# Softmax layers of a graph network: dense products from two float32r parts, four dense regions, and the border between gathered and dense nodes at 2750 in place of 3250

## What is computed

```python
msg = jax.nn.relu(x[src]) + EPS_MSG
m = jax.ops.segment_max(msg, dst, num_segments=n)
ex = jnp.exp(msg - m[dst])
alpha = ex / segment_sum(ex, dst, n)[dst]
out = segment_sum(msg * alpha, dst, n) + x
h = batch_norm(out @ W1 + b1);  x = relu(relu(h) @ W2 + b2)
```

## Time and profile before

| | |
|---|---|
| median of 3 runs | 4451.83 us (4436.73 to 4454.9) |
| the profiled execution | 4460.21 us, span 4458.4 us |
| TensorE, its weight loads | 3626.2 us (81%), 2451.3 us (55%) |
| GpSimd | 2568.9 us (58%) |
| VectorE, ScalarE | 1998.9 us (45%), 1185.7 us (27%) |
| DMA | 744.31 MB, 167 GB/s |
| setup, until the first gather | 749 us |
| softmax layers 1, 2, 3 with their nodes stages | 749 to 1478, 2230, 3006 us, about |
| edge layers | 3006 to 4425 us, about |

### The profile page before, as it was taken

The page is one execution under the profiler, slowest core; times in us unless marked ns, Lnnn a source line. Parts: engine busy times, 40 slices in busy tenths (PEclk is TensorE's granted clock), DMA queues, the critical chain, the costliest instruction groups (busy, mean ns, idle before and its releaser), DMA issues. The chain is left out here.

```text
span 4458.4 us, 73923 instructions
## 1 busy us (share of the span) xinstructions
PE 3626.2 (81%) x22631; PEld 2451.3 (55%) x22631; DVE 1998.9 (45%) x5297; ACT 1185.7 (27%) x2569; POOL 2568.9 (58%) x2700
## 2 busy tenths in 40 slices
PE   2588887889897888999687989876788788878887
PEld 0355554545555544555554555575666666666665
DVE  6354433122223712131641222374566666666666
ACT  1232111000001500000420000173444444444444
POOL 4566554556664665666475666536556565555552
PEclk6798988999998989999898999897898989899888
DMA  6365445666664766666376666464444444444442
GB/s 244 119 203 166 135 137 171 199 192 210 206 216 126 242 196 192 215 208 203 123 252 191 203 206 215 152 189 132 115 126 126 123 129 123 125 125 126 123 128 66
DMA packets 347311, 744.31 MB, mean 167 GB/s; under 512 B 73666, under 2 KB 177276, under 8 KB 346339
## 3 DMA queue, kind: packets, MB, share of 16 engines
q0 software_dynamic: 134912, 331.04, 25.7%
q1 hardware_dynamic: 204295, 358.83, 25.1%
q10 hardware_dynamic: 7899, 51.90, 3.0%
HBM read 608.06 MB, written 133.44 MB: 166 GB/s over the span
## 5 line engine op out<-in xcount | busy, mean ns | idle before, releaser
L603 POOL DMA_INDIRECT ring<-split_table,src_idx x1240 | 1179.4, 951 | 735.0 <-issue 334.9
L1488 PE MATMUL ps<-spare,acc 128*128 128x500 fp8e4 x5292 | 1229.3, 385 | 201.1 <-issue 97.9
L2117 POOL DMA_INDIRECT ring<-h_table,idx_ring x832 | 822.3, 988 | 581.2 <-issue 276.1
L1488 PEld LDWEIGHTS ps<-spare,acc 128*128 128x128 bf16 x5292 | 521.0, 100 | 850.0 <-issue 280.2
L1589 DVE TENSOR_TENSOR onehot<-onehot,ps 128x168 f32<-128x168 f32 x165 | 54.3, 329 | 1268.9 <-PE ps L1499 775.0
L616 POOL DMA_INDIRECT adjacency<-acc x408 | 403.0, 988 | 308.3 <-issue 112.8
L1433 ACT ACTIVATE work<-ps 84x256 f32<-84x256 f32 x155 | 58.9, 380 | 1744.1 <-remote 1305.2
L1520 PE MATMUL ps<-ring,onehot 128*84 128x256 bf16 x3720 | 469.1, 281 | 47.1 <-issue 46.3
L1520 PEld LDWEIGHTS ps<-ring,onehot 128*84 128x84 bf16 x3720 | 416.0, 122 | 73.5 <-issue 69.5
L2127 PE MATMUL ps<-ident,ring 128*128 128x128 f32 x1664 | 296.7, 302 | 99.0 <-issue 74.1
L2166 PEld LDWEIGHTS ps<-mats,work 128*128 128x128 f32 x1664 | 244.8, 208 | 167.7 <-issue 166.1
(11 more groups left out here) (328 smaller groups left out, 4920.3 us busy)
## 6 DMA issues: line engine op xcount, KB each, us to landing
acc<-split_table SPq DMA_DIRECT2D x104, 768.0 KB
spare<-adjacency SPq DMA_DIRECT2D x108, 512.0 KB
e_few<-spare SPq DMA_DIRECT2D x104, 512.0 KB
acc<-e_few SPq DMA_DIRECT2D x208, 256.0 KB
work<-in_edge_attr SPq DMA_DIRECT2D x104, 256.0 KB
split_table<-acc ACTq DMA_DIRECT2D x32, 768.0 KB
ring<-split_table,src_idx POOLq DMA_INDIRECT x1240
adjacency<-Z ACTq DMA_DIRECT2D x6, 3136.0 KB
```

The costliest lines, as they stand in the source:

```text
L603: e.indirect_dma_start(out=to, out_offset=None, in_=table, in_offset=bass.IndirectOffsetOnAxis(ap=src_idx[:, 2 * i + h, j:j + 1], axis=0)) ...
L1488: ins = e.matmul(ps[2 + 2 * c + kind][:, 0:width], split[j % 2][:, k, q, kind * D:(kind + 1) * D], moving, start=(b == q == 0), stop=(b == ...
L2117: e.indirect_dma_start(out=rows[:, s, j, :], out_offset=None, in_=h_table, in_offset=bass.IndirectOffsetOnAxis(ap=idx_ring[:, s, j:j + 1], ...
```

## The change

- The border goes to 2750: 46 pairs in place of 55, 250 nodes at a time as before; the dense part has 3500 nodes in four regions, of 1000, 1000, 1000 and 500. Setup scatters 476 columns in place of 408 and zeroes half a region more.
- The dense products no longer use the split table. ScalarE casts a block's counts from fp8 to float32r (`cast_block`, five buffers) and makes exp(x - c) of two blocks at a time (`dense_exp`), VectorE multiplies (`dense_times`), ScalarE rounds to a float32r high part (`dense_high`), VectorE subtracts to get the low part. TensorE multiplies 2 kinds x 2 parts per chunk: 8 matmuls for a block of 1000 columns, 4116 in the kernel.
- ScalarE and VectorE do this at the end of each step for the blocks of the next one. TensorE's blocks start at step 4 and fill 4130 columns a step.
- SyncE loads plain rows (256 KB a unit) in place of the split rows (768 KB), behind `d_mul`, and counts behind `cast`. In layers 2 and 3 the first dense work waits for the whole split table and its stores (`space_made`), since it takes over their memory.
- The gathered pairs keep the split table and their three bf16 parts.

```diff
-CUT = 3250
-PAIRS = 55
+CUT = 2750
+PAIRS = 46
 WHOLE = 5
 SLOTS3 = 3
-GROUP0 = 106
+GROUP0 = 89
 COLS = (NG - GROUP0) * J
...
-REGIONS = [(0, [500, 500]), (1000, [500, 500]), (2000, [500, 500])]
-STEP_BLOCKS = 2.75
+REGIONS = [(0, [500, 500]), (1000, [500, 500]), (2000, [500, 500]), (3000, [500])]
+CHUNKS = sum(len(widths) for _, widths in REGIONS)
+DUOS = -(-BLOCKS // 2)
+CASTS = 5
+FIRST_STEP = 4
+STEP_COLUMNS = 4130
...
 
-    return max(0, int((n - 3) / STEP_BLOCKS))
+    r, b = divmod(n, BLOCKS)
+    before = sum(BLOCKS * sum(widths) for _, widths in REGIONS[0:r]) + b * sum(REGIONS[r][1])
+    return FIRST_STEP + before // STEP_COLUMNS
...
+                            whole_rows = sum(REGIONS[r][1]) > PITCH // 2
+                            if whole_rows:
+                                e.dma_start(adjacency[at:at + half, :].rearrange("(p x) o -> p (x o)", p=P),
+                                            Z0[:, 0:half // P // 4].bitcast(U8)).then_inc(S("zero_fill"), 16)
+                            else:
+                                half_rows = adjacency[r * SPAN * PITCH:r * SPAN * PITCH + NR * PITCH, :].rearrange("(p b d) o -> p b (d o)", b=BLOCKS, d=PITCH)
+                                at = slice(h * BLOCKS // 2, (h + 1) * BLOCKS // 2)
+                                zeros = Z0[:, 0:(at.stop - at.start) * PITCH // 8].bitcast(U8).rearrange("p (b d) -> p b d", d=PITCH // 2)
+                                e.dma_start(half_rows[:, at, 0:PITCH // 2], zeros).then_inc(S("zero_fill"), 16)
...
+            def space_made(e, S):
+                if not ready:
+                    e.wait_ge(S("v_low"), UNITS)
+                    for b in range(5):
+                        e.wait_ge(S(f"split_out{b}"), stored_units(max(u for u in range(UNITS) if made_in(u) == b)))
...
+                    width = sum(REGIONS[r][1])
+                    if j >= 2:
+                        e.wait_ge(S("cast"), last_block(j - 2))
...
+                def load_dense_rows(j):
+                    u = j % UNITS
                     n = blocks_of(u)
-                    reached(e, S("dense"), j - 1)
-                    if not ready and j < 4:
-                        e.wait_ge(S(f"split_out{j - 2}"), 16)
-                    if not ready and r == 0:
-                        e.wait_ge(S(f"split_out{made_in(u)}"), stored_units(u))
-                    e.dma_start(split[j % 2][:, 0:n, :, :].rearrange("p n q x -> p n (q x)"), split_by_block[:, u * UNIT:u * UNIT + n, :]
-                                ).then_inc(S(f"split_in{j % 2}"), 16)
-
+                    if j >= 2:
+                        e.wait_ge(S("d_mul"), duos_through(j - 2))
+                    e.dma_start(dense_rows[j % 2][:, 0:n, :], by_block[:, u * UNIT:u * UNIT + n, :]).then_inc(S(f"dense_rows_in{j % 2}"), 16)
...
+                def dense_exp(d):
+                    n = first_block(d)
+                    j, k = unit_of(n), n % BLOCKS % UNIT
+                    m = end_block(d) - n
+                    if d == 0:
+                        space_made(e, S)
+                    if k == 0:
+                        e.wait_ge(S(f"dense_rows_in{j % 2}"), 16 * (j // 2 + 1))
+                    reached(e, S("d_low"), d - 1)
+                    e.activation(dense_values[d % 2][:, 0:m, 0:D], dense_rows[j % 2][:, k:k + m, :], ACT.Exp, bias=negc[:, :]
+                                 ).then_inc(S("d_exp"), 1)
+
+                def dense_high(d):
+                    m = end_block(d) - first_block(d)
+                    e.wait_ge(S("d_mul"), d + 1)
+                    if d >= 2:
+                        e.wait_ge(S("dense"), end_block(d - 2))
+                    e.activation(two_parts[:, d % 2, 0:m, 0, :], dense_values[d % 2][:, 0:m, :], ACT.Copy).then_inc(S("d_high"), 1)
+
+                def cast_block(n):
+                    r = n // BLOCKS
+                    j, k = unit_of(n), n % BLOCKS % UNIT
+                    width = sum(REGIONS[r][1])
+                    if k == 0:
+                        e.wait_ge(S(f"counts_in{j % 2}"), 16 * (j // 2 + 1))
+                    reached(e, S("dense"), n - CASTS + 1)
+                    e.activation(cast_counts[n % CASTS][:, 0:width], counts[j % 2][:, k, 0:width].bitcast(F8), ACT.Copy).then_inc(S("cast"), 1)
+
+                def keep_products(r):
+                    for c, width in enumerate(REGIONS[r][1]):
+                        e.wait_ge(S("dense"), BLOCKS * (r + 1))
+                        reached(e, S("evacuated"), 2 * (r - 1) + c + 1)
+                        e.activation(products[c][:, 0:width], ps[3 + 2 * c][:, 0:width], ACT.Copy).then_inc(S("product_kept"), 1)
+
+                def dense_duo(d):
+                    if d == 0:
+                        dense_exp(0)
+                    if d + 1 < ALL_DUOS:
+                        dense_exp(d + 1)
+                    if d > DUOS and d % DUOS == 1:
+                        keep_products(d // DUOS - 1)
+                    cast_block(first_block(d))
+                    dense_high(d)
+                    for n in range(first_block(d) + 1, end_block(d)):
+                        cast_block(n)
+
                 if not ready:
                     exp_rows(0)
...
+                    d = r * DUOS + b // 2
+                    e.wait_ge(S("d_low"), d + 1)
...
+                            for q in range(2):
+                                ins = e.matmul(ps[2 + 2 * c + kind][:, 0:width], two_parts[:, d % 2, b % 2, q, kind * D:(kind + 1) * D],
+                                               cast_counts[n % CASTS][:, at:at + width], start=(b == q == 0), stop=(b == BLOCKS - 1 and q == 1))
                         at += width
-                    if k == blocks_of(u) - 1:
-                        ins.then_inc(S("dense"), 1)
+                    ins.then_inc(S("dense"), 1)
...
+                def dense_times(d):
+                    n = first_block(d)
+                    j, k = unit_of(n), n % BLOCKS % UNIT
+                    m = end_block(d) - n
+                    e.wait_ge(S("d_exp"), d + 1)
+                    e.scalar_tensor_tensor(out=dense_values[d % 2][:, 0:m, D:2 * D], in0=dense_rows[j % 2][:, k:k + m, :], scalar=EPS_MSG,
+                                           in1=dense_values[d % 2][:, 0:m, 0:D], op0=ALU.add, op1=ALU.mult).then_inc(S("d_mul"), 1)
+
+                def dense_duo(d):
+                    m = end_block(d) - first_block(d)
+                    if d == 0:
+                        dense_times(0)
+                    if d + 1 < ALL_DUOS:
+                        dense_times(d + 1)
+                    if d > DUOS and d % DUOS == 1:
+                        keep_divisors(d // DUOS - 1)
+                    e.wait_ge(S("d_high"), d + 1)
+                    e.tensor_tensor(two_parts[:, d % 2, 0:m, 1, :], dense_values[d % 2][:, 0:m, :], two_parts[:, d % 2, 0:m, 0, :].bitcast(F32),
+                                    ALU.subtract).then_inc(S("d_low"), 1)
```

136 lines of the change are left out of this document (70 added, 66 removed).

## The result

The changed kernel took 4259.86 us (median of 4 runs, 4245.95 to 4262.09), the kernel before beside it 4453.36. The ratio is 0.9566, with a 95% interval of 0.9538 to 0.9593: 4.3% faster. The forecast was 4215 us. The profiled execution took 4259.97 us (span 4258.2) against 4460.21, so it moved by 200.2 us where the sum had 236.5.

What follows compares the result with a forecast made beforehand. GpSimd's gather bursts plus about 1.9 us of waiting bound the layers, TensorE second. Pairs -326.5, ScalarE +15, setup +75 sum to -236.5 us: 4223.7 by the profile, 4215 us as median; range 4150 to 4370.

Steps and rivals of the forecast that it cites:

- a burst plus about 1.9 us: Softmax layers' period per pair: eight gathers, 10.0 us, then GpSimd waits for the pair's sums; 11.9 us.
- The price of float32r: Dense products on TensorE: 0.23 us per 500-column matmul, bounds 0.21 and 0.31, so its step stays under the period.
- Rival A: Dense products: a float32r matmul costs 0.31 us, TensorE becomes the bound, 4530 us, slower than before; chance 0.09.
- The pairs saved: Softmax layers: the period paid 46 times instead of 55, gains of 116.3, 104.8 and 105.4 us, -326.5 in all.
- ScalarE in the last region: Last dense region: ScalarE's work of 12.5 us a step exceeds the period; 5 us a layer, +15 in all.
- nothing else waits: VectorE's added work, 2.3 us a step, 4.6 in the last region: losing its cover would only lengthen ScalarE's chain.
- rival B: Cast chain between ScalarE and VectorE: hand-offs and waits add 36 us a layer, 4320 us; chance 0.12.
- The start of layers 2 and 3: First gather from the split table starts where it does now, after five whole pairs; no cost priced.
- Setup: Stage before the layers: 68 more scatters +64 us, larger zero fill ahead 11 us; together +75.
- What follows the layers: Stages after the three softmax layers: no change forecast, 0 us.
- Rival C: Softmax layers: the 1.9 us go, the period falls to TensorE's 10.75 us, -160 us, 4055 us; chance 0.07.
- Rival D: Dense products run as true FP32: +21 us a step, near 6800 us; chance 0.02.

Runs made afterwards that it cites:

- a fourth slot: Changed kernel with four slots for gathered pairs in place of three, split table cut to two parts: 4243.75 us, 0.9605 of the kernel before.
- the pieces: Changed kernel with VectorE's reciprocal of 500 divisors cut into four of 125, one before each duo of dense blocks: 3630.84 us, 0.9876, prompt chip.
- the edit that undoes it: Changed kernel with dense work starting at step 5 in place of 4, 4240 columns a step: 3653.47 us, 0.9956, prompt chip.
- the gap: One or two extra small gathers behind each pair's eight, late chip: kernel before 4840.66 us (1.094), changed kernel 4508.19 us (1.019).

## Why the prediction was right or wrong

**The bound was read right for its chip, and the size of the gain hangs on that chip.** On the late chips the period is a burst and a dead time of 1.9 us, TensorE is second in line, and both ways of breaking that (a longer burst, a fourth slot) left the dead time in place. What I put down to the kernel, "a burst plus about 1.9 us", is half kernel and half chip: on a prompt chip the dead time isn't there and the kernel before is bound by TensorE. That the number came out has luck in it: no rival had the chip in it, and on a prompt chip the change was worth 16 us (3669.46 less 3653.26) where 236.5 were forecast.

**The price of float32r: right.** 0.23 us was taken from the sum over five instructions in the earlier trace rows, and it is 0.23. Rival A, by the raw 0.32 us, is out. The page TensorE: Matmul & The Clock Gate of the Trainium skill (Weight-path perf modes) says that fast weight loads are off for FP32. The rows agree, with loads of 192 ns against 98, but as forecast most of that lies under the matmuls, so the slower load didn't speak against the change. The load is also longer than the 0.11 us into which the prediction let a float32 one fit: in the trace of before the loads of L2148 take 213 ns in the mean, and overlap.

**The pairs saved: right in size.** 46 periods for 55. In layer 1 the 36 periods between the fourth sums and the 40th take 12.14 us in the mean, where 12.06 was taken: 2.9 us. The start was mis-sized. The first sums came 26.9 us after the first gather where 31.9 was said, but the next three periods took 43.2 us in place of 36.2, together +2.

**ScalarE in the last region: the term was too small and the engine half right.** The four steps from the 40th sums to the 44th took 57.5 us, 9.3 over 4 x 12.06, where 5 was allowed, and the tail behind them 2.2 more than said. I had priced ScalarE's chain, and it is shorter than said: in the trace a duo of the last region takes 2.3 to 2.4 us where 2.8 was worked out. What I had called covered was VectorE, "nothing else waits". TensorE does wait for it: the whole reciprocal now stands between the dense work and the adding up of a pair, and the pieces showed that. On top of that wait the pair's matmuls stand at half clock, which the sum didn't have. This is a part of rival B's price, in a way that B didn't name.

**The start of layers 2 and 3: a step that failed.** "I let the first gather from the split table start where it does" was wrong in layer 3. The first sums of a split pair came 116.1 us after the stage's first gather, where it was 101.0 before, and in layer 2 105.2 for 102.5. The last paragraph of the prediction had named the mechanism (the fifth exponential behind dense work) without a price. In layer 3 the first sums come 15 us later on the late chip, and in layer 2, where the fifth exponential is 16.7 us behind the fourth, 3 us later; on the prompt chip the edit that undoes it gave 3 to 4 us a layer.

**Setup: right within 7 us.** The first block moved from 164.8 to 174.2, 9.4 where 11 was said; that the zero fill is the cause wasn't tested by itself. The last block went from 743.8 to 764.1, 20.3 in all where 11 and 7 were said, so from first to last block the pairs lost 10.9 where 7 was said. The larger part of the 7 us is the tail: 49 scatters start behind the last block and not 44, since one more group of four and the end of another were still to be issued, and it lasts 61.0 us where 1 and 55.4 were said.

**What follows the layers** fell by 7.9 us, though the change doesn't touch it. Between the two traces with the gap, on another late chip, it fell by 11.1; between the prompt chip's two it is 1.3 us longer. No run tells its cause.

**Rival C** needed the dead time to hang on TensorE's stream. It hangs on the chip and on GpSimd's bursts. Rival D is out with A.

## What to carry to other kernels

The value of moving work off an engine is its price where it is the bound, so what a border between two methods is worth depends on the chip: nine pairs fewer with the cheaper products are worth 4.3% on one and 0.6% on another, and on the second kind, without the cheaper products, they cost 5%. Time the kernel before on the same chip, or the two can't be compared. An engine that is busy 43% of a layer, as VectorE here, still sets steps when a long instruction of it stands between two others that wait for each other: cut it before you count on its cover, and look at the granted clock behind the wait too. And work that an engine does alone behind all other work isn't won by moving it beside that work, if the two slow each other.

## What the runs showed that was not expected

Semaphores of TensorE's matmuls are told 0.01 us behind the modelled end of the matmul (median of the 155 telling matmuls of L1520) on a prompt chip, and 5.0 us behind it on a late one. ScalarE's reads say the same: in layer 1 they start 0.04 us behind that end on the prompt chip and 5.1 us on the late one (medians of 55). Semaphores of ScalarE and VectorE have a median of 0.01 us in the softmax layers also on a late chip. In steady state the delay ends, for most pairs, 1.5 to 2.4 us behind GpSimd's last gather of a burst, whether the burst has 8, 9 or 10.

The nodes stages, without gathers, have 0.01 us on both kinds of chip, and the first two last 39.6 us each on the late chip and 38.9 and 39.6 on the prompt one. All other stages have indirect DMAs of GpSimd, and all are longer on the late chip: the setup 749 us against 600, the three layers 690, 691 and 687 against 579, 584 and 592, and what follows them 1562 against 1239. The kernel before is 21% longer there in all (4453 us against 3671). That fits the delay; that the delay makes all of it was not shown. Slower DMA engines are not the cause: the packets of the gathers and scatters took 25.7% of 4458 us and 30.5% of 3673 us of the 16 engines' time, which is 1146 and 1120 us. The granted clock is lower on the late chip (0.895 against 0.960), and no run tells how much of the difference that is, nor whether it is more than a result of TensorE's waits.

One caution: the late chip's trace of the kernel before holds 30710 records of semaphore updates where the prompt chip's holds 77145, for the same 73923 instructions. So medians over semaphores on a late chip rest on the records that were kept; starts of instructions, as those of ScalarE's reads above, don't depend on them. Why records are missing is open.

The page Perfetto Trace Analysis of the Trainium skill (Tensor Engine Instruction (MATMUL, LD_WEIGHTS)) says that the recorded end of a matmul is estimated, and that the semaphore goes out once PSUM has acknowledged the writes and is then propagated. By that account the delay lies in the acknowledgement or in the propagation, and no run here tells in which. Whether it is the chip or something that shared it stays open too.
